# A GRU with an expert-choice layer on one Trainium2 core: the threshold search unrolled, its rounds refilled, its ties summed in one PSUM tile

## The chip, the cores and the metric

The kernel runs on one core of a Trainium2 chip. A core has a matrix engine (PE, or TensorE; its weight loads are shown as PEld), a vector engine (DVE, VectorE), an activation engine (ACT, ScalarE), a general engine (POOL, GpSimd), a queue engine (SP, SyncE) and 16 DMA engines that all the queues share. The engines run side by side and wait for each other through semaphores. The metric is the device time of one execution in microseconds (us), given as the median of three runs.

## The reference

A GRU cell runs over 256 rows of 16 sequences, with width D = 512. Its hidden states are the tokens of an expert-choice layer: each of 16 experts takes the 256 tokens (one in 16) with the highest softmax score, all of them go through one matrix, and the result, weighted by the score, is added to the input.

```python
gi = x @ W_ih + b_ih;  gh = h @ W_hh + b_hh
r = sigmoid(i_r + h_r);  z = sigmoid(i_z + h_z);  n = tanh(i_n + r * h_n)
h_new = (1.0 - z) * n + z * h                       # 256 steps, one after another
...
S = softmax(xf @ router_w + router_b, axis=-1)      # 4096 tokens, 16 experts
G, idx = top_k(S.T, 256)                            # ties go to the lower token index
out = einsum('ekh,hd->ekd', xf[idx], expert_w) + expert_b
y = zeros(...).at[idx.reshape(-1)].add(G[..., None] * out)
return x + y
```

Since all experts share one matrix, the kernel computes `tok @ expert_w + expert_b` for every token, and multiplies each token by the sum of the scores with which experts chose it.

## The kernel before

**Recurrence.** The first 1024 us or so are the 256 steps. A step is 64 matmul records of the recurrence on PE, in two halves, tanh on ACT, the gate arithmetic on DVE; PE fills its time with the input projections of later steps, with router matmuls and with expert matmuls.

**Tokens.** They lie in 32 tiles of 128 tokens by 512. An **expert unit** is a quarter of one 128-deep slice of one tile's expert product: one unit is 128 columns, 16 units make a tile. `expert(units, widest)` (L908 to L926) issues the next units in order, on PE's queue; four units at a quarter boundary go as one 512-wide group. Tiles 12 to 15 are computed in pairs by `paired` (56 units), tiles 16 to 30 follow with 16 units each, and `last_tile` does tile 31 in two halves. A plain tile starts by waiting for `ffn_preset` (L921): ACT has copied the bias into its PSUM bank (`preset_ffn`, L518 to L524). ACT moves nine finished tiles out of PSUM into SBUF (`store_ffn`, L526 to L537), so that their banks come free; the others stay in PSUM until the end.

**The search.** Top-k is done as a threshold search on the score's bits. Seven rounds find the upper 16 bits, eight the lower 16. A round r is a chain over three engines:

- DVE counts two candidates (L1378, each a pass over 512 columns and an accumulator read), ACT counts the third (`count_third`, L666 to L669);
- PE sums the counts per expert with a small matmul (`sum_counts`, L1038 to L1041, matmul at L1034), waiting for ACT's count (`cnt_act`) and DVE's (`cnt_own`);
- DVE compares (`reach`, L1394), makes new candidates (L1405), moves the threshold (L1399) and counts again; while PE works, it prepares steps and bases (`prepare`, L1382 to L1389).

Behind every sum PE issues nine units, so that it has work while DVE and ACT count. On DVE, rounds 1 to 6 are a hardware loop of three turns (L1416) and rounds 8 to 13 another (L1454), two rounds in a turn. The first round's counts are taken quarter by quarter (`count_first`, L1304 to L1312), the first three during the recurrence, the last right after the last softmax; each quarter's scores are first copied to an array of upper halves (L1302), which is what is counted.

Between the two halves, and again at the end, ACT makes one more count (`count_beyond`, L671 to L675) and PE sums it (`sum_beyond`, L1043 to L1047). ACT also does, round by round, one preset or one store (L677 to L701).

**Ties.** After the last round DVE marks scores that equal the threshold, runs a prefix sum over 512 columns (L1468), and takes the number of ties per segment, `R`. PE sums `R` over all groups of an expert and over the groups before, in two sums (L1071 and L1072). DVE subtracts (`others`, L1481), scans (`scan_b`, L1483), subtracts again (`fit`, L1484), and compares each token's rank with what fits (L1492). PE sums the chosen scores into token weights (L1078), a pair of quarters at a time.

**The end.** DVE makes `result = product * weight + x` for all 32 tiles in the order `OUT_ORDER` (`add_x`, L1518 to L1530), SP and ACT issue the stores in turn, and the last tile goes in halves (L1548, L1550). In `OUT_ORDER` eleven places (`PSUM_PLACES`) hold tiles read from PSUM.

Each engine's order is written out by hand; nothing is scheduled by a planner.

Of the kernel before, what the change touches and what calls it, by code (L numbers as in the profile page):

```python
# [5 lines left out]
def gru_expert_choice_kernel(nc, x, cond, w_ih, w_hh, b_ih, b_hh, router_w, router_b, expert_w, expert_b, out):  # L6
# [85 lines left out]
    PSUM_PLACES = [0, 1, 2, 4, 9, 14, 19, 23, 28, 30, 31]  # L92
# [19 lines left out]
    with ctx:  # L112
# [100 lines left out]
        before = sb("before", [P, P], F16)  # L213
        group_of = sb("group_of", [P, NI])
# [20 lines left out]
        R = sb("R", [P, SEG], F16)  # L235
        others = sb("others", [P, 1 + SEG])
        scan_b = sb("scan_b", [P, SEG])
# [9 lines left out]
        R_total_ps = gates[1][1][:, 0:SEG]  # L247
        R_before_ps = gates[1][1][:, SEG:2 * SEG]
# [98 lines left out]
        cnt_act = sem("cnt_act")  # L347
        first_own = sem("first_own")
# [79 lines left out]
        def _(pool):  # L428
# [19 lines left out]
            then_step(nc.gpsimd.memset(before[:, :], 0.0))  # L448
            then_step(nc.gpsimd.memset(group_of[:, :], 1.0))
# [3 lines left out]
            by_group = before[:, :].rearrange("p (j h e) -> p j h e", j=J, h=2)  # L453
            for j in range(J):
# [12 lines left out]
        def _(act):  # L467
# [140 lines left out]
            def count_first_third(g):  # L608
                cols = slice(g * P, (g + 1) * P)
                act.wait_ge(cand_ready, 1)  # L610
                act.wait_ge(key_ready, g + 1)
                nc.scalar.activation(junk_first[:, 0:P], upper[:, cols], ACT.Sign, bias=cand[:, 2:3],
# [64 lines left out]
            for r in range(1, UPPER_ROUNDS + LOWER_ROUNDS + 1):  # L677
# [10 lines left out]
                elif r % 2 and r <= 11:  # L688
                    preset_ffn(PLAIN + r // 2)
                elif r <= 10:  # L690
                    store_ffn(IN_LOOP + r // 2 - 2)
                elif r == 12:
                    store_ffn(PLAIN)
                    preset_ffn(PLAIN + BANKS)
                elif r == 13:
                    store_ffn(PLAIN + 1)
                elif r == 14:
                    preset_ffn(PLAIN + BANKS + 1)
                else:
                    store_ffn(PLAIN + 2)  # L700
# [872 lines left out]
```

## Time and profile before

| | us |
|---|---|
| median of 3 runs (lowest, highest) | 1099.16 (1098.94, 1100.22) |
| the profiled execution | 1098.95 |
| its span in the trace | 1096.8 |
| PE busy | 1085.3 (99%) |
| DVE busy | 857.9 (78%) |
| ACT busy | 411.7 (38%) |
| granted PE clock | 0.998 of full speed |

The profiled execution lies 2.15 us above its span, and 0.21 us below the median. PE's busy time is an upper bound: matmuls are pipelined, and the end of one is modelled. The last 70 us, from 1027 us of the span on, hold the search (15 rounds, to 1061), the ties (to 1067), and then the 32 tile results with their stores. The chain of waits runs through PE for 94% of the span; in the search it runs through DVE.

### The profile page before, as it was taken

The page shows a single profiled execution, that of the slowest core. Times are in us where ns is not written, and L with a number is a line of the kernel's source. Part 1 is how long each engine was busy: PE and PEld are TensorE (multiplying, and loading weights), DVE is VectorE, ACT ScalarE, POOL GpSimd, SP SyncE. Part 2 cuts the span into 40 slices and gives each one's busy share as a digit, 9 for nine tenths or more (in the row PEclk, how much of TensorE's full clock was granted, in tenths as well). Part 3 has the DMA queues.
Part 4 walks back from the last instruction along what each step waited for, and adds up shares of the span by engine and source line. Part 5 has one row for each costly group of instructions (what it writes and reads, how often), then busy time and mean ns, then how long its engine had stood idle before and what let it go on. Part 6 is the DMA issues. An engine that isn't in the chain of part 4 may idle for free.

```text
span 1096.8 us, 60944 instructions
## 1 busy us (share of the span) xinstructions
PE 1085.3 (99%) x26728; PEld 895.2 (82%) x26728; DVE 857.9 (78%) x4603; ACT 411.7 (38%) x1658; POOL 6.9 (1%) x31
## 2 busy tenths in 40 slices
PE   8999999999999999999999999999999999999998
PEld 5788888888888888888888888888888888888742
DVE  5788777877777877787777778778788777777897
ACT  2333333433333433333333334343334333333461
POOL 2000000000000000000000000000000000000000
PEclk9999999999999999999999999999999999999999
DMA  7311000000000000000000000000000000000359
GB/s 255 90 22 23 13 13 13 7 10 13 14 13 13 14 13 9 8 13 13 13 13 14 13 9 8 13 14 13 13 13 14 7 10 14 3 4 4 113 161 307
DMA packets 80446, 36.78 MB, mean 34 GB/s; under 512 B 70051, under 2 KB 70307, under 8 KB 80182
## 3 DMA queue, kind: packets, MB, share of 16 engines
q1 hardware_dynamic: 77840, 28.79, 10.7%
q8 instruction: 209, 3.42, 1.3%
q10 hardware_dynamic: 2342, 4.11, 1.1%
q14 instruction: 55, 0.45, 0.1%
HBM read 24.49 MB, written 8.39 MB: 30 GB/s over the span
## 4 chain that ended last, share of the span: by engine, by line
PE 94%; DVE 3%; DMA 1%; issue 0%; SPq 0%; ACT 0%; DVEq 0%
PE gates L805 60%; PE gates L742 26%; PE ffn_ps L869 3%; PE gates L923 2%; DMA whh<-in_L_cond_W_hh 1%; DVE wih L1378 1%; PE gates L901 1%; PE log_ps L958 1%; PE ffn_ps L923 0%; PE gates L935 0%; DVE reached L1394 0%; SPq L375 0%; PE log_ps L1034 0%; PE ffn_ps L901 0%; SPq L378 0%
## 5 line engine op out<-in xcount | busy, mean ns | idle before, releaser
L805 PE MATMUL gates<-whh,tok 128*16 128x192 f32 x16384 | 713.9, 326 | 3.1 <-DVE tok L1187 2.0
L805 PEld LDWEIGHTS gates<-whh,tok 128*16 128x16 f32 x16384 | 566.2, 124 | 101.0 <-DVE tok L1187 3.9
L511 ACT ACTIVATE th<-gates 128x128 f32<-128x128 f32 x512 | 140.0, 274 | 340.8 <-PE gates L805 340.6
L1162 DVE SCALAR_TENSOR_TENSOR u<-th,gates 128x64 f32<-128x64 f32 x512 | 113.2, 221 | 166.4 <-ACT th L511 166.2
L516 ACT ACTIVATE n_t<-v 128x64 f32<-128x64 f32 x512 | 131.5, 257 | 278.2 <-DVE v L1166 278.2
L742 PE MATMUL gates<-wih,xS 128*32 128x192 f32 x3024 | 146.2, 326 | 0.0
L1178 DVE STREAM_TRANSPOSE nT<-n_t 128x64 f32<-128x64 f32 x512 | 123.6, 241 | 0.0
L1169 DVE STREAM_TRANSPOSE zT<-th 128x64 f32<-128x64 f32 x512 | 121.9, 238 | 0.0
L1166 DVE SCALAR_TENSOR_TENSOR v<-u,gates 128x64 f32<-128x64 f32 x512 | 113.1, 221 | 8.8
L742 PEld LDWEIGHTS gates<-wih,xS 128*32 128x32 f32 x3024 | 99.9, 110 | 21.1
L1187 DVE SCALAR_TENSOR_TENSOR tok<-new_n,z_h 128x32 f32<-128x32 f32 x512 | 110.1, 215 | 8.7
L1174 DVE SCALAR_TENSOR_TENSOR z_h<-zT,half_h 128x32 f32<-128x32 f32 x512 | 98.6, 193 | 17.6
L742 PE MATMUL gates<-wih,xT 128*32 128x192 f32 x2016 | 105.3, 326 | 0.0
L1182 DVE SCALAR_TENSOR_TENSOR new_n<-zT,nT 128x32 f32<-128x32 f32 x512 | 96.7, 189 | 8.8
L742 PEld LDWEIGHTS gates<-wih,xT 128*32 128x32 f32 x2016 | 66.6, 110 | 13.4
L1206 DVE TENSOR_SCALAR half_h<-tok 128x64 f32<-128x64 f32 x255 | 57.6, 226 | 8.7
L742 PE MATMUL gates<-w_sums,xT 128*32 128x192 f32 x1008 | 52.6, 326 | 0.0
L742 PE MATMUL gates<-w_sums,xS 128*32 128x192 f32 x1008 | 52.6, 326 | 0.0
L476 ACT ACTIVATE gates<-bias 128x256 f32<-128x256 f32 x128 | 47.8, 374 | 0.0
L923 PE MATMUL gates<-we,tok 128*32 128x128 f32 (+1 forms) x648 | 44.7, 419 | 0.0
L742 PEld LDWEIGHTS gates<-w_sums,xS 128*32 128x32 f32 x1008 | 33.3, 110 | 7.7
L742 PEld LDWEIGHTS gates<-w_sums,xT 128*32 128x32 f32 x1008 | 33.3, 110 | 7.6
(198 smaller groups left out, 615.9 us busy)
## 6 DMA issues: line engine op xcount, KB each, us to landing
x_in<-in_x SPq DMA_DIRECT2D x248, 32.0 KB, 2.1
out<-tok SPq DMA_DIRECT2D x16, 256.0 KB, 4.2
xs<-in_x SPq DMA_DIRECT2D x14, 256.0 KB, 3.6
out<-tok ACTq DMA_DIRECT2D x13, 256.0 KB, 4.5
wih<-in_L_cond_W_ih SPq DMA_DIRECT2D x4, 768.0 KB, 7.7
whh<-in_L_cond_W_hh SPq DMA_DIRECT2D x4, 768.0 KB, 13.3
whh<-in_x SPq DMA_DIRECT2D x12, 256.0 KB, 3.6
we<-in_L_ffn_expert_w SPq DMA_DIRECT2D x4, 256.0 KB, 2.7
```

What stands on the lines that cost most here:

```text
L511: nc.scalar.activation(th[a][:, :, :].rearrange("p g c -> p (g c)"), gates[t // S % PAIRS][a][:, R_:HN], ACT.Tanh, scale=0.5).then_inc(th_ ...
L516: nc.scalar.activation(n_t[a][:, :], v[a][:, :], ACT.Tanh).then_inc(n_ready[a], 1)
L742: mm = nc.tensor.matmul(ps[Q * j:Q * (j + 1), IN:HN].rearrange("b (g k c) -> b g k c", g=G, k=KH), rows(k), columns(k, j), start=False, st ...
L805: mm = nc.tensor.matmul(gates[t // S % PAIRS][a][Q * j:Q * j + rows, R_:GC].rearrange("b (g k c) -> b g k c", g=G, k=KH), columns, by_tile ...
L923: mm = nc.tensor.matmul(bank(n)[Q * j:Q * (j + 1), cols], tile(n)[:, kc * P + Q * j:kc * P + Q * (j + 1)], we[:, kc, cols], start=False, s ...
L1162: V.scalar_tensor_tensor(u[a][:, :], th[a][:, 0, :], 1.0, ps[a][:, HN:GC], ALU.add, ALU.mult).then_inc(u_ready[a], 1)
L1166: V.scalar_tensor_tensor(v[a][:, :], u[a][:, :], 0.5, ps[a][:, IN:R_], ALU.mult, ALU.add).then_inc(v_ready[a], 1)
L1169: V.transpose(zT[a][:, :, :].rearrange("p k q -> p (k q)"), th[a][:, 1, :]).then_inc(zT_ready[a], 1)
L1174: V.scalar_tensor_tensor(z_h[a][:, :, :], zT[a][:, :, rows], 1.0, half_h[:, chunks[a], :], ALU.add, ALU.mult)
L1178: V.transpose(nT[a][:, :, :].rearrange("p k q -> p (k q)"), n_t[a][:, :]).then_inc(nT_ready[a], 1)
L1182: V.scalar_tensor_tensor(new_n[a][:, :, :], zT[a][:, :, rows], 1.0, nT[a][:, :, rows], ALU.subtract, ALU.mult).then_inc(new_n_ready[a], 1)
L1187: V.scalar_tensor_tensor(by_chunk[:, chunks[a]], new_n[a][:, :, :], -0.5, z_h[a][:, :, :], ALU.mult, ALU.add).then_inc(h_ready[a], 1)
```

## The change

Six things change.

1. Both hardware loops of the search are unrolled on DVE.
2. PE issues ten units in a round instead of nine, through `fill_round`: all but one, then the wait for ACT's next count, then the last. `sum_counts` waits for DVE's count alone.
3. In the first quarter counts, the last quarter is counted where the scores lie (every second 16-bit half), by DVE and by ACT; the copy of the upper halves follows the counts.
4. Ties: a second mask, `behind`, is the transposed order of `before`; both products are summed into one PSUM tile, of `R` and of `R` shifted by one segment. DVE scans that tile directly: two subtractions go.
5. ACT counts `beyond` ahead of `side` in the last round, and the stores and presets of rounds 10 to 15 are spread anew; the units around `sum_beyond` and the ties become 8 and 2, 6 and 6 (from 8 and 6, 8 and 6).
6. `PSUM_PLACES` changes, and the router bias is added in step 22 instead of step 16.

```diff
-    LAST_UNITS, SOFTMAX_UNITS, ROUND_UNITS = [3, 6, 4, 5], 17, 9
-    BEYOND_UNITS, TIE_UNITS = [[7, 5], [8, 6]], [8, 6]
+    LAST_UNITS, SOFTMAX_UNITS, ROUND_UNITS = [3, 6, 4, 5], 17, 10
+    BEYOND_UNITS, TIE_UNITS = [[7, 5], [8, 2]], [6, 6]
-    PSUM_PLACES = [0, 1, 2, 4, 9, 14, 19, 23, 28, 30, 31]
+    PSUM_PLACES = [0, 1, 2, 3, 7, 12, 17, 22, 27, 30, 31]
...
+                    if j:
+                        then_step(fill(by_group_behind[:, 0:j, hi, :], [j], p))
+                    if hi == 1:
+                        then_step(fill(by_group_behind[:, :, 0, :], [J], p))
...
             def count_third(r, key):
                 act.wait_ge(cand_ready, r)
+                if r == 2:
+                    act.wait_ge(key_ready, NG)
...
-                elif r % 2 and r <= 11:
+                elif r % 2 and r <= 9:
                     preset_ffn(PLAIN + r // 2)
                 elif r <= 10:
                     store_ffn(IN_LOOP + r // 2 - 2)
+                    if r == 10:
+                        preset_ffn(PLAIN + BANKS - 1)
+                elif r == 11:
+                    store_ffn(PLAIN)
                 elif r == 12:
-                    store_ffn(PLAIN)
                     preset_ffn(PLAIN + BANKS)
+                    store_ffn(PLAIN + 1)
                 elif r == 13:
-                    store_ffn(PLAIN + 1)
-                elif r == 14:
                     preset_ffn(PLAIN + BANKS + 1)
                 else:
-                    store_ffn(PLAIN + 2)
-                    preset_ffn(PLAIN + BANKS + 2)
+                    store_ffn(PLAIN + r - 12)
+                    preset_ffn(PLAIN + BANKS + r - 12)
+            count_beyond(1, lower)
...
-            count_beyond(1, lower)
-            store_ffn(IN_PSUM - 2)
-            preset_ffn(IN_PSUM + BANKS - 2)
...
+            def fill_round(units, third):
+                expert(units - 1, widest=4)
                 pe.wait_ge(cnt_act, third - 1)
+                expert(1)
+
+            def sum_counts(r):
                 pe.wait_ge(cnt_own, r - 1)
                 sum_by_expert(cnt_ps, cnt[:, :]).then_inc(cnt_all, 1)
...
-            sum_by_expert(R_total_ps, R[:, :])
-            sum_by_expert(R_before_ps, R[:, :], before).then_inc(R_summed, 1)
+            for j in range(J):
+                for mask, of in ((behind, R_earlier), (before, R)):
+                    mm = nc.tensor.matmul(ties_ps[Q * j:Q * (j + 1), :], mask[:, Q * j:Q * (j + 1)], of,
+                                          start=(mask is behind), stop=(mask is before), skip_group_check=True)
+            mm.then_inc(R_summed, 1)
...
-                count = V.tensor_scalar(junk_first[:, (c + 1) * P:(c + 2) * P], upper[:, cols], cand[:, c:c + 1], None, ALU.is_ge,
+                key = S_halves[:, cols, 1] if g == NG - 1 else upper[:, cols]
+                count = V.tensor_scalar(junk_first[:, (c + 1) * P:(c + 2) * P], key, cand[:, c:c + 1], None, ALU.is_ge,
...
-                if t == 2 * TT:
+                if t == 3 * TT - 2:
...
+            copy_upper(NG - 1)
+            dve.wait_ge(key_ready, NG)
...
-            with dve.Fori(0, (UPPER_ROUNDS - 1) // 2) as q:
+            for q in range((UPPER_ROUNDS - 1) // 2):
...
-            with dve.Fori(0, (LOWER_ROUNDS - 1) // 2) as q:
+            for q in range((LOWER_ROUNDS - 1) // 2):
...
-            link(V.tensor_tensor(others[:, 1:], R_total_ps, R[:, :], ALU.subtract))
-
-            link(V.tensor_tensor_scan(scan_b[:, :], zeros[:, :], others[:, 0:SEG], need[:, 0:1], ALU.add, ALU.subtract))
-            link(V.tensor_tensor(fit[:, :], scan_b[:, :], R_before_ps, ALU.subtract))
+            dve.wait_ge(soft, need_set)
+
+            link(V.tensor_tensor_scan(fit[:, :], zeros[:, :], ties_ps, need[:, 0:1], ALU.add, ALU.subtract))
```

PE's order in rounds 8 and 9, before. Rows of 32x3 are the sums of counts; rows of 32x128 and 32x512 are expert units (4 matmuls each for one unit and for four).

```order
L1034 MATMUL log_ps<-cnt,same_expert 32x3 [waits cnt_own,cnt_act]
L1034 MATMUL log_ps<-cnt,same_expert 32x3 x3
L923 MATMUL gates<-we,tok 32x128 x8
L923 MATMUL gates<-we,tok 32x512 x4
L923 MATMUL gates<-we,tok 32x128 x12
L1034 MATMUL log_ps<-cnt,same_expert 32x3 [waits cnt_own,cnt_act]
L1034 MATMUL log_ps<-cnt,same_expert 32x3 x3
L923 MATMUL gates<-we,tok 32x128 x4
L923 MATMUL gates<-we,tok 32x512 x4
L923 MATMUL gates<-we,tok 32x512 [waits ffn_preset]
```

And now, from the sum of round 8 to the sum of round 9:

```order
L1048 MATMUL log_ps<-cnt,same_expert 32x3 [waits cnt_own]
L1048 MATMUL log_ps<-cnt,same_expert 32x3 x3
L937 MATMUL gates<-we,tok 32x512 x8
L937 MATMUL gates<-we,tok 32x128 [waits ffn_preset]
L937 MATMUL gates<-we,tok 32x128 x3
L937 MATMUL gates<-we,tok 32x128 [waits cnt_act]
L937 MATMUL gates<-we,tok 32x128 x3
L1048 MATMUL log_ps<-cnt,same_expert 32x3 [waits cnt_own]
```

The fifth plain tile (tile 20) starts with unit 120. Before, that was the sixth unit behind the sum of round 9; now it is the ninth behind the sum of round 8, and its wait for `ffn_preset` stands ahead of the sum of round 9.

DVE's order from the first row of the tie count to the comparisons, before:

```order
L1469 TENSOR_TENSOR R<-wih 128x64 [waits soft]
L1472 SCALAR_TENSOR_TENSOR wih<-wih 128x512 [waits side_ready]
L1474 TENSOR_SCALAR need<-log_ps,need_base 128x1 [waits cnt_all]
L1481 TENSOR_TENSOR others<-gates,R 128x64 [waits half_taken,half_added,xs_loaded3,R_ready,xs_loaded2,R_summed,xs_loaded1,xs_loaded0]
L1483 SCALAR_TENSOR_TENSOR scan_b<-zeros,need,others 128x64 [waits soft]
L1484 TENSOR_TENSOR fit<-scan_b,gates 128x64 [waits soft]
L1492 TENSOR_TENSOR wih<-wih,fit 128x16x8 [waits soft]
```

And now:

```order
L1508 TENSOR_TENSOR R_padded<-wih 128x64 [waits soft]
L1511 SCALAR_TENSOR_TENSOR wih<-wih 128x512 [waits side_ready]
L1513 TENSOR_SCALAR need<-log_ps,need_base 128x1 [waits cnt_all]
L1522 SCALAR_TENSOR_TENSOR fit<-zeros,need,gates 128x64 [waits half_added,half_taken,R_ready,xs_loaded3,R_summed,xs_loaded2,soft,xs_loaded1,xs_loaded0]
L1530 TENSOR_TENSOR wih<-wih,fit 128x16x8 [waits soft]
```

One instruction stands where three stood, and the wait for PE's sum of ties (`R_summed`) has moved to it.

## Rows read from the trace of the kernel before

**Rows 1.** Windows, the search: busy us of each engine, clock, DMA.
```profile
core 0: us, PE busy (x) PEld busy (x) DVE busy (x) ACT busy (x) POOL busy (x), PEclk, DMA share, GB/s
1027.30:1063.20 35.90, 33.18 (x700) 17.84 (x692) 33.19 (x194) 22.23 (x53) 0.00 (x0) 1.00 0.68 200
```
**Rows 2.** Timeline, PE: start us, us, engine line op, names [idle before].
```profile
1029.35 0.19 PE L1034 MATMUL log_ps<-cnt,same_expert 128*32 128x3 f16 x4
...
1036.43 0.19 PE L1034 MATMUL log_ps<-cnt,same_expert 128*32 128x3 f16 x4
...
1038.94 0.19 PE L1034 MATMUL log_ps<-cnt,same_expert 128*32 128x3 f16 x4 [0.35 <-DVE wih L1378]
...
1041.22 0.19 PE L1034 MATMUL log_ps<-cnt,same_expert 128*32 128x3 f16 x4
...
1044.56 0.19 PE L1034 MATMUL log_ps<-cnt,same_expert 128*32 128x3 f16 x4 [0.23 <-DVE wih L1378]
...
1046.94 0.19 PE L1034 MATMUL log_ps<-cnt,same_expert 128*32 128x3 f16 x4 [0.21 <-DVE wih L1378]
...
1060.80 0.19 PE L1034 MATMUL log_ps<-cnt,same_expert 128*32 128x3 f16 x4
1060.83 1.93 PE L923 MATMUL ffn_ps<-we,tok 128*32 128x128 f32 x40
```
**Rows 3.** Timeline, DVE: the comparison behind a sum.
```profile
1036.91 0.16 DVE L1394 SCALAR_TENSOR_TENSOR reached<-log_ps,target 128x3 f32<-128x3 f32 x1 [0.35 <-PE log_ps L1034]
...
1047.18 0.16 DVE L1394 SCALAR_TENSOR_TENSOR reached<-log_ps,target 128x3 f32<-128x3 f32 x1
```
**Rows 4.** Timeline, ACT: count and preset behind the sum at 1044.56.
```profile
1045.37 0.72 ACT L668 ACTIVATE wih<-wih,cand 128x512 uint16<-128x512 uint16 x1 [1.02 <-DVE cand L1405]
...
1046.09 0.58 ACT L524 ACTIVATE gates<-be 128x512 f32<-128x512 f32 x1
```
**Rows 5.** Counts on DVE by source line: ns minimum/median/maximum.
```profile
L1378 DVE TENSOR_SCALAR_CACHE_REDUCE wih<-upper_bits,cand x12: 737/741/745, 1027.8 to 1040.3; 128x512 uint16<-128x512 uint16 x12
```
```profile
L1309 DVE TENSOR_SCALAR_CACHE_REDUCE junk_first<-upper_bits,cand x8: 304/340/346, 466.7 to 1026.6; 128x128 uint16<-128x128 uint16 x8
```
**Rows 6.** Timeline, DVE: the ties.
```profile
1063.41 0.28 DVE L1469 TENSOR_TENSOR R<-wih 128x64 f16<-128x64 f32 x1
...
1064.21 0.21 DVE L1474 TENSOR_SCALAR need<-log_ps,need_base 128x1 f32<-128x1 f32 x1
1065.01 0.23 DVE L1481 TENSOR_TENSOR others<-gates,R 128x64 f32<-128x64 f32 x1 [0.59 <-PE gates L1034]
1065.28 0.35 DVE L1483 TENSOR_TENSOR_SCAN scan_b<-zeros,need,others 128x64 f32<-128x64 f32 x1
1065.66 0.22 DVE L1484 TENSOR_TENSOR fit<-scan_b,gates 128x64 f32<-128x64 f32 x1
1065.92 0.49 DVE L1492 TENSOR_TENSOR wih<-wih,fit 128x128 f32<-128x128 f32 x2
```
**Rows 7.** Timeline, ACT: side and beyond after the last round.
```profile
1061.76 0.72 ACT L704 ACTIVATE wih<-scores_by_expert,edge 128x512 f32<-128x512 f32 x1 [0.61 <-DVE edge L1464]
1062.39 0.71 ACT L674 ACTIVATE wih<-wih,beyond 128x512 uint16<-128x512 uint16 x1
1063.00 0.19 ACT L674 ACTIVATION_READ_ACCUMULATOR wih<-wih,beyond 128x1 f16 x1
```
**Rows 8.** Timeline, DVE: tile 30 and the first half of tile 31.
```profile
1090.20 0.75 DVE L1528 SCALAR_TENSOR_TENSOR tok<-gates,weight,w_sums 128x512 f32<-128x512 f32 x1 [0.67 <-PE gates L923]
1091.92 0.48 DVE L1548 SCALAR_TENSOR_TENSOR w_sums<-gates,weight,w_sums 128x256 f32<-128x256 f32 x1 [0.98 <-PE gates L935]
```
**Rows 9.** DMA issues from 1090 us (KB each, us to landing); windows near the end.
```profile
out<-tok ACTq DMA_DIRECT2D x1, 256.0 KB, 4.5
...
out<-w_sums SPq DMA_DIRECT2D x1, 128.0 KB, 2.3
```
```profile
1094.50:1095.50 1.00, 0.00 (x0) 0.00 (x0) 0.00 (x0) 0.00 (x0) 0.00 (x0) 1.00 0.19 54
```
**Rows 10.** The page: the recurrence's matmuls and PE's idle time before them.
```profile
L805 PE MATMUL gates<-whh,tok 128*16 128x192 f32 x16384 | 713.9, 326 | 3.1 <-DVE tok L1187 2.0
```

More of the change, by code:

```diff
@@ L213, in gru_expert_choice_kernel @@
         before = sb("before", [P, P], F16)
+        behind = sb("behind", [P, P], F16)
         group_of = sb("group_of", [P, NI])
@@ L234, in gru_expert_choice_kernel @@
         need = sb("need", [P, 1])
-        R = sb("R", [P, SEG], F16)
-        others = sb("others", [P, 1 + SEG])
-        scan_b = sb("scan_b", [P, SEG])
+        R_padded = sb("R_padded", [P, 1 + SEG], F16)
+        R, R_earlier = R_padded[:, 1:], R_padded[:, 0:SEG]
         fit = sb("fit", [P, SEG])
@@ L448, in _ @@
             then_step(nc.gpsimd.memset(before[:, :], 0.0))
+            then_step(nc.gpsimd.memset(behind[:, :], 0.0))
             then_step(nc.gpsimd.memset(group_of[:, :], 1.0))
@@ L453, in _ @@
             by_group = before[:, :].rearrange("p (j h e) -> p j h e", j=J, h=2)
+            by_group_behind = behind[:, :].rearrange("p (j h e) -> p j h e", j=J, h=2)
             for j in range(J):
@@ L610, in count_first_third @@
                 act.wait_ge(cand_ready, 1)
-                act.wait_ge(key_ready, g + 1)
-                nc.scalar.activation(junk_first[:, 0:P], upper[:, cols], ACT.Sign, bias=cand[:, 2:3],
+                if g < NG - 1:
+                    act.wait_ge(key_ready, g + 1)
+                    key = upper[:, cols]
+                else:
+                    act.wait_ge(scored, 1)
+                    key = Sc.bitcast(U16).rearrange("p (n two) -> p n two", two=2)[:, cols, 1]
+                nc.scalar.activation(junk_first[:, 0:P], key, ACT.Sign, bias=cand[:, 2:3],
                                      accum_out=cnt_first[:, g, 2:3]).then_inc(first_act, 1)
@@ L1046, in sum_beyond @@
                 sum_by_expert(cnt_beyond_ps[half], cnt_beyond[:, half:half + 1]).then_inc(cnt_all, 1)
-                expert(BEYOND_UNITS[half][1], widest=4)
             pe.wait_ge(masks_ready, 1)
@@ L1300, in soften, with copy_upper @@
                 if i == 6:
-                    link(V.transpose(Sc[:, cols], by_token_scores[:, :]))
-                    V.tensor_copy(upper[:, cols], S_halves[:, cols, 1]).then_inc(key_ready, 1)
+                    turned = V.transpose(Sc[:, cols], by_token_scores[:, :])
+                    if g == NG - 1:
+                        turned.then_inc(scored, 1)
+                        dve.wait_ge(scored, 1)
+                    else:
+                        link(turned)
+                    if g < NG - 1:
+                        copy_upper(g)
+            def copy_upper(g):
+                cols = slice(g * P, (g + 1) * P)
+                V.tensor_copy(upper[:, cols], S_halves[:, cols, 1]).then_inc(key_ready, 1)
             def count_first(g, c):
                 cols = slice(g * P, (g + 1) * P)
-                dve.wait_ge(key_ready, g + 1)
+                if g < NG - 1:
+                    dve.wait_ge(key_ready, g + 1)
                 dve.wait_ge(cand_ready, 1)
-                count = V.tensor_scalar(junk_first[:, (c + 1) * P:(c + 2) * P], upper[:, cols], cand[:, c:c + 1], None, ALU.is_ge,
+                key = S_halves[:, cols, 1] if g == NG - 1 else upper[:, cols]
+                count = V.tensor_scalar(junk_first[:, (c + 1) * P:(c + 2) * P], key, cand[:, c:c + 1], None, ALU.is_ge,
                                         ALU.add, accum_out=cnt_first[:, g, c:c + 1])
@@ L1439, in _ @@
             V.memset(no_prefix, 0.0)
-            V.memset(others[:, 0:1], 0.0)
+            V.memset(R_padded[:, 0:1], 0.0)
             dve.wait_ge(cand_ready, UPPER_ROUNDS + 1)
@@ L1473, in _ @@
             dve.wait_ge(cnt_all, ALL_ROUNDS + 2)
-            mark(V.tensor_scalar(need[:, :], cnt_beyond_ps[1], -0.5, need_base[:, :], ALU.mult, ALU.add))
+            need_set = mark(V.tensor_scalar(need[:, :], cnt_beyond_ps[1], -0.5, need_base[:, :], ALU.mult, ALU.add))
             for p in range(4):
```

23 lines of the change are left out of this document (12 added, 11 removed).

## The prediction

> **What bounds the kernel now.** I began with the page. PE is busy for 99% of the span, and its only idle time in the recurrence is 3.1 us over 256 steps [rows 10]. So the change can only act behind the recurrence. Next came the windows. In the search, from 1027.3 to 1063.2, PE counts as busy for 33.18 of 35.90 us and DVE for 33.19 [rows 1]: two engines hand work to each other, and both are short of full by 2.7 us. Then PE's timeline, for the distance from one sum of counts to the next. Where no loop boundary lies between, it is 2.28 us (1038.94 to 1041.22). From 1036.43 to 1038.94 it is 2.51, and PE then stood idle for 0.35 us until DVE's count came [rows 2]. DVE's timeline shows why: the comparison starts 0.24 us behind its sum in the plain case (1046.94, 1047.18), but 0.48 us behind the sum at 1036.43, where the loop turns [rows 2, 3]. Hence in the search DVE's chain sets the pace, and PE's expert units are filler. At the end it is the other way round: DVE waits for PE before tile 30 (0.67 us) and before the first half of tile 31 (0.98 us) [rows 8].
>
> The total of expert units is the same. PE therefore ends earlier by what it no longer idles. That is two things: how much earlier the search and the ties end (call it D), and how many units were moved from behind them into the idle time.
>
> **Unrolling.** Sums 2 to 7 span 1029.35 to 1041.22, 11.87 us for five rounds; at 2.28 each this would be 11.40: 0.47 us less. Sums 9 to 15 span 1046.94 to 1060.80, 13.86 us; six times 2.28 is 13.68: 0.18 less [rows 2]. Sum 0.65 us. It can't be much more, since the plain round stays, and it can be nothing if code without a loop stalls elsewhere.
>
> The Trainium skill ("Advanced Engine Details and Errata", Control Flow Timing) gives a compare-and-branch about 108 ns. By that figure four boundaries would be worth an estimated 0.43 us instead of 0.65. The trace agrees for a lower boundary and shows twice as much for the upper one that I quote; the rows decide.
>
> **Ten units in a round.** Eight units take 1.93 us with a tail of 0.19 that the sums show too, so a unit is (1.93 - 0.19) / 8 = 0.218 us [rows 2]. Ten are 2.18, and 0.03 for the sum ahead of them makes 2.21: under 2.28, by 0.07. DVE stays the pace-maker, barely. ACT's count, now waited for before the tenth unit, ends some 1.7 us behind a sum (1045.37 + 0.72 + 0.19 for the accumulator, less 1044.56) [rows 2, 4, 7], while the tenth unit is due at 1.98. So this wait is free. Behind it on PE's queue stand only the last unit and the sum.
>
> **One round gets a new wait.** The order rows show tile 20 starting as the ninth unit behind sum 8, with a wait for `ffn_preset`. PE gets there at 0.03 + 8 x 0.218 = 1.77 us behind the sum. ACT issues that preset in its round 9, right behind the count: 1046.09 + 0.58 = 1046.67, which is 2.11 us behind sum 8 [rows 2, 4]. Its place on ACT has not changed. PE stands still for 0.34 us, then does two units (0.44) and sums at about 2.60, instead of 2.38 before (1044.56 to 1046.94). DVE has long finished and waits too. Cost: 0.22 to 0.3 us, I take 0.25. The other plain tiles start at units 72, 88, 104, 136, 152, 168, 184 and 200, and each preset of theirs is issued at least a round ahead or right at the round's start; I cost these at nothing, and each that I have wrong costs up to the same 0.34.
>
> **The last quarter counted in place.** The copy leaves the way to the first comparison, but comes back just before `prepare`, which the comparison needs in order. The transposed scores, two counts, one copy and four preparations stand on DVE before and after; only the order differs. Sum 1 may come a little earlier, the comparison doesn't. I take 0, between -0.1 and +0.2. Is a strided 16-bit read slower? The dense count takes 340 ns for 128 elements and 741 for 512 [rows 5]: 401 ns for 384, 1.04 ns an element.
>
> The Trainium skill ("VectorE: DVE Perf Modes", What auto-detection actually checks) has a double rate for 16-bit tensors with step 1, by which the dense count would be fast and the strided one lose it. The trace shows no such rate in the dense count, so nothing is lost; by the rule, two counts would each lose an estimated 0.07 us.
>
> **Ties.** All times from sum 15 at s = 1060.80. Before, DVE has `need` started at s + 3.41, waits 0.59 us for PE's sums of R, and goes through `others`, the scan and `fit` to the comparisons at s + 5.12 [rows 6]. PE was late since ACT made `side` ahead of `beyond`: the count ended at 1063.00 + 0.19, s + 2.39 [rows 7], and then six units (1.31) stood ahead of the sum of R. Now ACT's `beyond` starts where `side` started, s + 0.96, and ends at about s + 1.77; PE has its eight units done by s + 1.77, sums, does two units by s + 2.25 and is ready for R, which DVE writes from s + 2.61 to s + 2.89 [rows 6]. R is summed by s + 3.25, `side` ends by s + 2.5, and neither is late for DVE. `need` ends at s + 3.62, the scan starts at s + 3.66; from the start of the scan to the next instruction it took 0.38 before (1065.28 to 1065.66). The comparisons start at s + 4.04: 1.08 us earlier. Reading PSUM in the scan instead of SBUF is not in the trace; `others` read PSUM and cost 0.27 from start to start, so I bound it by 0 and 0.2.
>
> So D = 0.65 - 0.25 + 0 + 1.08 = 1.48 us, from 0.9 to 1.9.
>
> **Units moved.** Ten instead of nine in 13 rounds are 13 more; the second `sum_beyond` has four fewer and the ties two fewer behind it: 7 more by the time of the weights, 7 x 0.218 = 1.5 us less for PE behind them. PE ends 1.48 + 1.5 = 3.0 us earlier. DVE's tile results start D earlier and had 0.67 + 0.98 = 1.65 us to spare for the 1.5 that PE gains on them [rows 8]: enough by 0.15. The new `PSUM_PLACES` keep the tiles in PSUM at places where their products and the bank presets are ready.
>
> **Stores.** These start only D earlier. Before, a 256 KB store near the end took 4.5 us to land and the last, of 128 KB, 2.3 [rows 9]: the queue was full, and had drained for the last one. From 1094.5 to 1095.5 the DMA engines were 0.19 busy [rows 9], so there is about 0.8 us of air ahead of the last half, plus what the late tile 30 opened before it. The stores can thus end 1.48 + 0.8 = 2.3 to 2.9 us earlier, PE 3.0. The later one counts. I take 2.7.
>
> **Other parts.** The bias add moves from step 16 to step 22, beside work with slack both times, as PE's idle time there is nothing; POOL builds one mask more in the first 20 us, needed 1000 us later. ACT's store and preset in one round add up to 0.72 + 0.19 + 2 x 0.58 = 2.07 us, less than 2.28. Each at nothing.
>
> **Sum.** 1098.95 - 2.7 = 1096.25 for an execution like the profiled one, which lies 0.2 below the median: 1096.5 us. A measurement of this kernel can tell about 0.2%, 2.2 us, from no change; 1096.96 is that border.
>
> **Rivals.**
>
> *The stores set the end.* If the queue of stores is full to its last byte, the end moves by D alone, plus nothing for the units moved: 1099.16 - 1.5 = 1097.7. For it: 4.5 us of landing. Against: the 0.19 window. Chance 0.2, and in steps between.
>
> *PE becomes the bound of the search.* The margin is 0.07 us a round. If ten units and a sum take 2.35, 11 rounds lose 0.07 each, 0.8 us of D, but PE then idles for nothing: PE ends at the same total, stores 0.8 later, giving 1097.3. For it: narrow units with a wait in between. Chance 0.12.
>
> *Fetching unrolled code (slower).* DVE runs 14 rounds of straight code in a stretch in which loads keep the DMA engines 0.68 busy [rows 1]. If the code comes in pieces over the same engines, and each piece takes as long as a queued transfer (4.5 us [rows 9]) with DVE standing, two such stops cost 9.0 us, of which 2.7 are covered: 1099.16 + 6.3 = 1105.5. It decides from one stop on (+1.8). Against: DVE and PE both run straight code through the whole recurrence and PE through this very search, and the idle times in the rows are below 0.6 us. Chance 0.05.
>
> The Trainium skill ("Advanced Engine Details and Errata", ISA Cache) speaks for this rival: it describes a store of two lines of 256 instructions each, which a two-round loop fits and unrolled code leaves. No row here shows such a stop.
>
> *The change doesn't do what it says.* Loop boundaries cost what they cost for another reason, the straight code keeps them: D is 0.65 smaller, 1097.1. Chance 0.05. The forecast itself keeps 0.58, with a range of its own from 1095.7 to 1097.0.
>
> **Chances.** Faster by over 0.2%: nearly all of the forecast, and near a third of the rivals that end at 1097: 0.62. Within 0.2%: 0.32. Slower: 0.06. The range for 8 in 10 is 1095.4 to 1098.6.
>
> **What would show it.** In the profile after: sums 2.28 us apart everywhere but from 8 to 9, where PE's weight loads wait for ACT's preset and the distance is about 2.6; the comparisons 4.04 us behind sum 15; PE's last matmul 3.0 us earlier; DVE without idle time before tile 30; the last store landing in more than 2.3 us. The forecast is wrong if sums come 2.35 or more apart, if other presets are waited for, or if DVE shows a stop with no engine named.

## The result, and the profile after

| us | before | after |
|---|---|---|
| median (lowest, highest) of 15 executions each, taken side by side | 1099.28 (1098.87, 1100.22) | 1095.98 (1095.10, 1097.74) |
| the profiled execution | 1098.95 | 1096.32 |
| its span | 1096.8 | 1094.6 |
| PE busy | 1085.3 | 1081.6 |

The kernel became faster: ratio after to before 0.9971, 95% interval 0.9964 to 0.9978, which is 3.2 us; the medians lie 3.3 us apart. The forecast was 1096.5.

The sums of counts and two rows at which PE waited (PE's timeline after; start, duration, idle time before in brackets; answers to [rows 2]):

```profile
1029.28 0.19 PE L1048 MATMUL log_ps<-cnt,same_expert 128*32 128x3 f16 x4
...
1036.00 0.19 PE L1048 MATMUL log_ps<-cnt,same_expert 128*32 128x3 f16 x4
1038.23 0.19 PE L1048 MATMUL log_ps<-cnt,same_expert 128*32 128x3 f16 x4
1040.44 0.19 PE L1048 MATMUL log_ps<-cnt,same_expert 128*32 128x3 f16 x4
...
1043.71 0.19 PE L1048 MATMUL log_ps<-cnt,same_expert 128*32 128x3 f16 x4
1045.86 0.64 PE L937 MATMUL gates<-we,tok 128*32 128x128 f32 x16 [0.20 <-ACT gates L531]
1046.32 0.19 PE L1048 MATMUL log_ps<-cnt,same_expert 128*32 128x3 f16 x4
...
1059.65 0.19 PE L1048 MATMUL log_ps<-cnt,same_expert 128*32 128x3 f16 x4
...
1062.61 0.22 PE L1094 MATMUL gates<-R_padded,behind 128*32 128x64 f16 x4 [0.52 <-DVE R_padded L1508]
```

Without a loop, neighbouring sums are 2.20 to 2.24 us apart (1036.00, 1038.23, 1040.44), not 2.28. Once, from sum 3 to sum 4, it is 2.29. Sum 2 to sum 15 takes 30.37 us; before it took 31.45. One stretch is long: 1043.71 to 1046.32, 2.61, with PE waiting for ACT's preset.

The ties on DVE's timeline after (answers to [rows 6]), and then DVE around tile 31 (answers to [rows 8]):

```profile
1062.28 0.28 DVE L1508 TENSOR_TENSOR R_padded<-wih 128x64 f16<-128x64 f32 x1
...
1063.07 0.21 DVE L1513 TENSOR_SCALAR need<-log_ps,need_base 128x1 f32<-128x1 f32 x1
1063.41 0.35 DVE L1522 TENSOR_TENSOR_SCAN fit<-zeros,need,gates 128x64 f32<-128x64 f32 x1
1063.80 0.49 DVE L1530 TENSOR_TENSOR wih<-wih,fit 128x128 f32<-128x128 f32 x2
...
1065.28 0.75 DVE L1566 SCALAR_TENSOR_TENSOR tok<-gates,weight,whh 128x512 f32<-128x512 f32 x1
...
1087.31 0.75 DVE L1566 SCALAR_TENSOR_TENSOR tok<-gates,weight,w_sums 128x512 f32<-128x512 f32 x1
1088.29 0.48 DVE L1586 SCALAR_TENSOR_TENSOR w_sums<-gates,weight,w_sums 128x256 f32<-128x256 f32 x1 [0.23 <-PE gates L949]
```

The comparisons start 4.15 us behind sum 15 (before 5.12), and the first tile result at 1065.28; before it started at 1067.39. That is D: 2.11 us. Tile 30 has no idle time ahead of it.

The last stores after (issues from 1088 us, us to landing), and the DMA engines to the end (windows of 1 us; answer to [rows 9]):

```profile
out<-tok ACTq DMA_DIRECT2D x1, 256.0 KB, 5.1
...
out<-w_sums SPq DMA_DIRECT2D x1, 128.0 KB, 3.6
```
```profile
1091.00:1092.00 1.00, 0.00 (x0) 0.00 (x0) 0.00 (x0) 0.00 (x0) 0.00 (x0) 1.00 1.00 310
1092.00:1093.00 1.00, 0.00 (x0) 0.00 (x0) 0.00 (x0) 0.00 (x0) 0.00 (x0) 0.86 0.91 294
1093.00:1094.00 1.00, 0.00 (x0) 0.00 (x0) 0.00 (x0) 0.00 (x0) 0.00 (x0) 0.50 0.30 100
```

The gap ahead of the last half is gone: the DMA engines are full to 1092 and 0.91 busy to 1093, and the last 128 KB take 3.6 us where they took 2.3. PE's last tile starts at 1086.31 (before 1089.94), the last store is issued at 1090.53 (before 1094.16). Both are 3.63 earlier; 1.3 of it is given back in the queue.

### The profile page after: what moved, and what is told of

It is laid out like the page before. It is cut to its first block, busy times and chain, and to the rows that moved or that the text cites. A ratio compares the mean times of both kernels' runs of the same rounds, so it can differ in the third digit from the quotient of the medians.

```text
span 1094.6 us, 60966 instructions
## 1 busy us (share of the span) xinstructions
PE 1081.6 (99%) x26752; PEld 892.5 (82%) x26752; DVE 857.2 (78%) x4601; ACT 411.3 (38%) x1658; POOL 15.5 (1%) x42
## 3 DMA queue, kind: packets, MB, share of 16 engines
q8 instruction: 209, 3.42, 1.3%
## 4 chain that ended last, share of the span: by engine, by line
PE 96%; DVE 1%; DMA 1%; SPq 0%; ACT 0%; issue 0%; DVEq 0%
PE gates L819 60%; PE gates L756 26%; PE ffn_ps L883 3%; PE gates L937 3%; DMA whh<-in_L_cond_W_hh 1%; PE gates L915 1%; PE ffn_ps L937 1%; PE log_ps L972 1%; PE gates L949 0%; DVE wih L1417 0%; SPq L376 0%; PE ffn_ps L915 0%; DVE u L1186 0%; SPq L379 0%; DVE wih L1507 0%
```

## The experiments

The comparison is with 1095.98 for the changed kernel, and with its trace. The kernel before, run beside them, had medians of 1099.24 to 1099.35. A profiled execution can be compared from sum 2 on; where it begins differs (last section).

**Experiment 1: the wait for ScalarE's count.** Ten units stay, the wait moves back to the sum.

```diff
                 expert(units - 1, widest=4)
-                pe.wait_ge(cnt_act, third - 1)
                 expert(1)
+                pe.wait_ge(cnt_act, third - 1)
```


> The changed kernel, with ScalarE's count waited for right ahead of the sum again (ten units, then both waits). Theory A: the second wait standing between the last unit and the sum costs about 0.06 us in each round, since after the change the distance from one sum to the next is 2.21 us where it was 2.28. Then the plain rounds come at 2.26 to 2.30 us here, sum 15 about 0.7 us later, and the whole 0.7 us slower. Rival: the rounds are shorter because PE no longer runs dry ahead of the sum (ten units fill it), and where the wait stands is worth nothing: 2.21 us and the same time as the changed kernel within 0.2 us.

Measured 1096.75 (ratio to before 0.9978, 0.9968 to 0.9987). PE's timeline of this kernel:

```profile
1036.24 0.19 PE L1048 MATMUL log_ps<-cnt,same_expert 128*32 128x3 f16 x4
1038.52 0.19 PE L1048 MATMUL log_ps<-cnt,same_expert 128*32 128x3 f16 x4
1040.79 0.19 PE L1048 MATMUL log_ps<-cnt,same_expert 128*32 128x3 f16 x4
```

The round is 2.27 to 2.28 again, and sum 2 to sum 15 takes 30.96: 0.59 us lost, about 0.05 in a plain round. Theory A held, though ACT's count had ended 0.76 us ahead of the sum (its accumulator read starts 0.95 ahead of it and takes 0.19). The profile shows no idle time for this wait. Where it sits shows from DVE's side: the last thing that the sum needs is DVE's second accumulator read, which in the changed kernel and in this one starts at

```profile
1038.09 0.09 DVE L1417 DVE_READ_ACCUMULATOR wih<-upper_bits,cand 128x1 f16 x1
```
```profile
1038.29 0.08 DVE L1417 DVE_READ_ACCUMULATOR wih<-upper_bits,cand 128x1 f16 x1
```

The sums behind them are at 1038.23 and 1038.52: 0.14 and 0.23 us later. With the wait at the sum it is 0.23 or 0.24 in every plain round, here and in the kernel before. With the wait moved it is 0.14 in a kernel with nine units (experiment 3) and 0.13 to 0.18 with ten, but for sum 9 behind the preset's stop. So the wait costs 0.09 us where it stands ahead of the sum, and ten units take part of that back.

**Experiment 2: the wait moved in the kernel before**, which keeps its loops and its nine units.

```diff
-            expert(ROUND_UNITS, widest=4)
+            fill_round(ROUND_UNITS, 2)
```


> The kernel before (loops, nine units) with ScalarE's count waited for ahead of the last unit and nothing else. By theory A each of 13 rounds is 0.06 to 0.08 us shorter, 2.19 to 2.21 us in the plain ones, sum 15 0.8 to 1.0 us earlier and the end 0.8 us. Rival: the shorter round needs the unrolled code as well: less than 0.3 us.

Measured 1098.59 (0.9994, 0.9985 to 1.0003), 0.65 under the kernel before and within the noise; the profiled execution was the slowest, 1100.16. Sum 2 to sum 15 went from 31.45 to 30.85, 0.60 less. But it is not the same gain in each round: seven rounds fell from 2.27 or 2.28 to 2.18 or 2.19 (1029.50 to 1031.68), 0.09 each, and the six in which a loop starts, turns or ends stayed where they were (2.54, 2.51, 3.34, 2.38, 2.38, 2.38). DVE's timeline at an upper boundary shows why, first before, then here:

```profile
1036.40 0.15 DVE L1389 SCALAR_TENSOR_TENSOR base<-steps,thr_away 128x1 f32<-128x1 f32 x1
1036.91 0.16 DVE L1394 SCALAR_TENSOR_TENSOR reached<-log_ps,target 128x3 f32<-128x3 f32 x1 [0.35 <-PE log_ps L1034]
```
```profile
1036.47 0.15 DVE L1394 SCALAR_TENSOR_TENSOR base<-steps,thr_away 128x1 f32<-128x1 f32 x1
1036.98 0.16 DVE L1399 SCALAR_TENSOR_TENSOR reached<-log_ps,target 128x3 f32<-128x3 f32 x1 [0.35 <-PE log_ps L1034]
```

The comparison starts 0.51 us behind the last preparation both times, though the sum (1036.43, 1036.41) came 0.23 and 0.14 behind the counts. Both rows name PE, but here DVE's own loop turn sets the comparison, and an earlier sum gains nothing. Experiment 1 found nearly the same total by other parts: about 0.05 in each of eleven plain rounds, with ten units.

**Experiment 3: nine units in the changed kernel.**

```diff
-    LAST_UNITS, SOFTMAX_UNITS, ROUND_UNITS = [3, 6, 4, 5], 17, 10
+    LAST_UNITS, SOFTMAX_UNITS, ROUND_UNITS = [3, 6, 4, 5], 17, 9
```


> The changed kernel with nine expert units in a round, everything else new. Theory A (the wait moved ahead of the last unit gives the shorter round): the rounds stay at 2.20 to 2.22 us though PE runs dry ahead of each sum, the round from sum 8 to 9 falls to 2.3, and PE's last matmul comes 13 x 0.214 = 2.8 us later less 0.35, near 1092.5 us; the end then is PE's again, about 1.5 us later than the changed kernel. Rival (a PE without gaps gives the shorter round): the rounds go back to 2.27 us, and everything comes 0.7 us later still.

Measured 1097.72 (0.9984, 0.9974 to 0.9993): 1.7 us slower than ten units; the profiled execution was the slowest, 1100.15. The sums come 2.18 to 2.19 apart, closer than with ten, so PE without gaps is not what shortened the rounds. Ten units make the round 0.035 us longer than nine. PE's last tile starts at 1090.44, 4.1 later than with ten. 13 units of 0.218 left for the end are 2.8. Sum 15 is 1.34 later: this execution's sum 2 came 0.68 later, the rounds are 0.64 shorter in all, and there is a stop of 1.30:

```profile
1032.14 0.18 PE L1048 MATMUL log_ps<-cnt,same_expert 128*32 128x3 f16 x3
1033.63 0.18 PE L1048 MATMUL log_ps<-cnt,same_expert 128*32 128x3 f16 x1 [1.30 <-issue]
```

PE stands between the third and the fourth matmul of one sum, and the row names no engine that it waited for. More on it below.

**Experiment 4: the loops put back** in the changed kernel.

```diff
-            for q in range((UPPER_ROUNDS - 1) // 2):
+            with dve.Fori(0, (UPPER_ROUNDS - 1) // 2) as q:
```
(and the same for the lower rounds)

> The changed kernel with both hardware loops on VectorE again. My price: 0.65 us, at two boundaries of the upper loop (0.23 to 0.26 us each) and two of the lower (about 0.1 each); sum 15 comes 0.5 to 0.7 us later and the end 0.5 to 0.7 us. Rival: with ten units PE covers part of a boundary: sum 15 under 0.3 us later.

Measured 1097.18 (0.9982, 0.9973 to 0.9992). DVE's timeline at two loop turns:

```profile
1031.93 0.16 DVE L1433 SCALAR_TENSOR_TENSOR reached<-log_ps,target 128x3 f32<-128x3 f32 x1 [0.38 <-PE log_ps L1048]
...
1036.64 0.16 DVE L1433 SCALAR_TENSOR_TENSOR reached<-log_ps,target 128x3 f32<-128x3 f32 x1 [0.35 <-PE log_ps L1048]
```

The sums ahead of them were at 1031.38 and 1036.09: 0.55 from sum to comparison, where the round after it has 0.24. Rounds with an upper boundary take 2.49 and 2.50, with a lower one 2.39 and 2.35. Sum 2 to 15 takes 31.27, 0.90 more than unrolled: more than the 0.65 expected, and the rival failed.

**Experiment 5: unrolling alone**, in the kernel before.

```diff
-            with dve.Fori(0, (UPPER_ROUNDS - 1) // 2) as q:
+            for q in range((UPPER_ROUNDS - 1) // 2):
```


> The kernel before with the two loops unrolled and nothing else. Price as in the prediction: sum 15 0.65 us earlier (0.23 to 0.26 at each of two upper boundaries, 0.1 at each of two lower ones), PE's last matmul as much, the end 0.5 to 0.7 us earlier. Putting the loops back into the changed kernel cost 0.90 us up to sum 15; by that rival 0.9 us here.

Measured 1098.56 (0.9993, 0.9984 to 1.0002), 0.7 under the median before and within the noise. Sum 2 to 15 takes 30.98, 0.47 less; but one of PE's sums in it is stretched:

```profile
1031.96 0.50 PE L1034 MATMUL log_ps<-cnt,same_expert 128*32 128x3 f16 x4
1034.53 0.19 PE L1034 MATMUL log_ps<-cnt,same_expert 128*32 128x3 f16 x4
```

Four matmuls that take 0.19 took 0.50, and the round 2.57. Without these 0.30 the unrolling would be worth an estimated 0.77. In the kernel before the same sum took 0.38, which cost nothing, since a loop boundary lay behind it. The plain round stays at 2.27 to 2.28, so it is not what shortened the rounds after.

**Experiment 6: the late preset issued a round earlier.**

```diff
+                elif r == 9:
+                    pass
...
+                    if r == 8:
+                        preset_ffn(PLAIN + BANKS - 2)
```


> The changed kernel with the bias preset of tile 20 one round earlier on ScalarE, behind the store of round 8, so that PE doesn't stop ahead of sum 9. Theory: the distance from sum 8 to sum 9 falls from 2.61 us to 2.35, everything behind it comes 0.25 us earlier, the stores too, and so the end: -0.25 us (-0.0 to -0.4), under what times alone can tell. Rival: the end doesn't follow, since something else sets it.

Measured 1095.96 (0.9969, 0.9958 to 0.9980). PE's sums 8 and 9:

```profile
1043.74 0.19 PE L1052 MATMUL log_ps<-cnt,same_expert 128*32 128x3 f16 x4
1046.01 0.19 PE L1052 MATMUL log_ps<-cnt,same_expert 128*32 128x3 f16 x4
```

The distance falls from 2.61 to 2.27, and sum 2 to 15 from 30.37 to 30.00. The stop was 0.34 to 0.37 us. The median did not move. In the trace PE's last tile and the last store (1090.24) start 0.29 earlier; a gain of 0.3 is less than these executions scatter, so whether the end follows stays open.

**Experiment 7: the old tie sums** in the changed kernel.

```diff
-            link(V.tensor_tensor_scan(fit[:, :], zeros[:, :], ties_ps, need[:, 0:1], ALU.add, ALU.subtract))
+            link(V.tensor_tensor(others[:, 1:], R_total_ps, R, ALU.subtract))
+            link(V.tensor_tensor_scan(scan_b[:, :], zeros[:, :], others[:, 0:SEG], need[:, 0:1], ALU.add, ALU.subtract))
+            link(V.tensor_tensor(fit[:, :], scan_b[:, :], R_before_ps, ALU.subtract))
...
```
(and on PE the two sums of the kernel before)

> The changed kernel with the old ties: two sums on PE, then subtract, scan, subtract on VectorE; the new order on ScalarE (beyond ahead of side) and the two units behind it stay. Of my 1.08 us for the ties, two instructions less are 0.26 + 0.26 us by their starts before, and the rest came from PE's sum being ready in time. Expected: from sum 15 to the comparisons 4.15 + 0.5 = 4.65 us, first tile result 0.5 us later, end 0.5 us later. Rival: the whole gain hangs on the single scan, and the comparisons come over 0.9 us later.

Measured 1096.76 (0.9979, 0.9968 to 0.9989). DVE's timeline:

```profile
1063.27 0.23 DVE L1522 TENSOR_TENSOR others<-gates,R_padded 128x64 f32<-128x64 f32 x1
1063.54 0.35 DVE L1523 TENSOR_TENSOR_SCAN scan_b<-zeros,need,others 128x64 f32<-128x64 f32 x1
1063.92 0.22 DVE L1524 TENSOR_TENSOR fit<-scan_b,gates 128x64 f32<-128x64 f32 x1
1064.17 0.49 DVE L1532 TENSOR_TENSOR wih<-wih,fit 128x128 f32<-128x128 f32 x2
```

Sum 15 is at 1059.51, so the comparisons start 4.66 behind it: 0.51 for the two subtractions. `others` shows no wait here. So of the 0.97 that the ties gained, 0.51 is the two subtractions. The other 0.46 is left to ACT's and PE's new order, which no run had by itself.

**Experiment 8: the copy back ahead of the counts** in the last quarter.

```diff
-                key = S_halves[:, cols, 1] if g == NG - 1 else upper[:, cols]
+                key = upper[:, cols]
...
```
(the copy goes ahead of the counts, and ACT counts the copy too)

> The changed kernel with the last quarter copied to the array of upper halves first and counted there, by VectorE and ScalarE, as before. I had counted this part at nothing: the first comparison then starts at the same distance behind the transposed scores, within 0.1 us (before 1.54, changed kernel 1.44), and the run is the same. Rival: the copy ahead of the counts costs its 0.23 us.

Measured 1096.79 (0.9976, 0.9967 to 0.9986), 0.8 over the changed kernel, with intervals that overlap. The trace supports less. From the transposed scores to the first comparison it has 1.55 us (1026.65, 1028.20), after 1.44 (1025.89, 1027.33), before 1.54; to sum 2 it has 3.53, 3.39 and 3.58. So counting in place is worth 0.11 to the comparison and 0.14 to sum 2. The rest of the difference in medians isn't in these rows; this execution began its recurrence 0.76 later (the second step at 24.38 against 23.62).

**Experiments 9 to 11: do the stores set the end?** Four of the last tile results (places 24 to 27) are computed and not stored, so these rows of the output are missing. After:

```diff
+                if i in (24, 26):
+                    continue
...
-                if i % 2:
+                if i % 2 and i not in (25, 27):
```


> The changed kernel without the stores of places 24 to 27 (1 MB of the output is not written). Leaving out places 12 to 15 only lowered the landing time of the last half from 3.6 to 3.0 us, since the queue filled again behind the hole. Theory S: with a late hole the queue is empty at the end, the last half lands 2.3 to 2.5 us after its issue, and the run is about 1.2 us shorter than the changed kernel, PE at its place. Rival: no more than 0.3 us shorter.

Before, with the same edit:

> The kernel before without the stores of places 24 to 27 (1 MB of the output is not written). Theory S: before the change the queue had drained by the last store (2.3 us to landing), PE set the end: under 0.2 us shorter. Rival: the stores already set the end before, and it is shorter by as much as the changed kernel is without the same stores.

And after with places 12 to 15 left out in their stead:

> The changed kernel without the stores of the results at places 12 to 15 (1 MB of the output is not written). Theory S: after the change the store queue sets the end (the last half lands 3.6 us after its issue, where it took 2.3 before); with four stores fewer it lands after 2.3 us again, and the run is 1.2 to 1.5 us shorter, PE's last matmul at the same place. Rival P: PE and the last result set the end, and the landing time is a side effect: no change within 0.3 us.

| not stored | us | ratio to before | last landing | median against the kernel with all stores |
|---|---|---|---|---|
| after, 24 to 27 | 1095.35 | 0.9963 (0.9950, 0.9975) | 2.3 | -0.6 |
| before, 24 to 27 | 1099.22 | 1.0000 (0.9990, 1.0009) | 2.3 | 0 |
| after, 12 to 15 | 1095.72 | 0.9966 (0.9954, 0.9979) | 3.0 | -0.3 |

The last landing after, without places 24 to 27 (issues from 1088 us, us to landing):

```profile
out<-w_sums SPq DMA_DIRECT2D x1, 128.0 KB, 2.3
```

Before, these stores cost nothing. After, the same edit takes the last landing from 3.6 to 2.3 and the span from 1094.6 to 1093.2. With places 12 to 15 left out the hole fills again: the DMA engines were 0.74 to 0.83 busy from 1076 to 1082 (windows of 2 us), and 0.98 and more from 1084 on. There the median fell by 0.3, where 1.2 to 1.5 was expected. Without places 24 to 27 it came out 0.6 shorter, where theory S wanted 1.2. Part of the rest is outside the span, where this kernel spends 2.0 to 2.1 us and the changed one 1.7 to 1.8; the spans' medians differ by 0.95 (1094.2, 1093.25). The medians' difference is about the size of the scatter, so this rests on the spans and the landings. One landing alone is a weak witness: in experiment 2, near the kernel before, the last half took 3.8 us in the one execution that was profiled. Within that, stores did not set the end before, and they hold it back now.

**Experiment 12: two tile results ahead of each second comparison**, with experiment 6 in it, so that the stores start sooner.

```diff
-    BEYOND_UNITS, TIE_UNITS = [[7, 5], [8, 2]], [6, 6]
+    BEYOND_UNITS, TIE_UNITS = [[7, 5], [8, 2]], [6, 9]
...
             add_x(0)
+            add_x(1)
             choose(QUARTERS[2])
             choose(QUARTERS[3])
-            add_x(1)
+            add_x(2)
+            add_x(3)
             take_weights(slice(2, 4))
...
```

> The changed kernel with the preset of tile 20 a round earlier, and on VectorE the results of places 0 and 1 ahead of the choice of the second pair of quarters, those of places 2 and 3 ahead of its weights (nine units on PE ahead of that pair's sums, not six). Since the stores set the end of the changed kernel, earlier first stores should count: 0.37 us from the preset as measured, and 0.2 to 0.4 from stores 1 to 3 coming 0.2 to 0.4 us earlier. Expected 0.5 to 0.8 us under the changed kernel: 1095.3. Rival: the queue's rate, not its start, sets its end, and only the 0.37 remain.

Measured 1097.02 (0.9979, 0.9970 to 0.9988), worse than the 1095.96 it was built on. Its search takes 31.49 us from sum 2 to 15 instead of 30.00, and PE's timeline says why:

```profile
1030.95 0.82 PE L941 MATMUL gates<-we,tok 128*32 128x128 f32 x19
1032.89 0.53 PE L941 MATMUL gates<-we,tok 128*32 128x128 f32 x11 [1.12 <-issue]
```

A stop of 1.12 us, again with no engine named, again at 1032; the other 0.37 of the difference lies in the same two rounds, from sum 2 to sum 4. Behind sum 15 the edit did a little: the third result starts 7.35 us behind it (1061.10, 1068.45), after 7.55 (1059.65, 1067.20). What it is worth without the stop stays open. The four fastest of its eleven executions, 1095.47 to 1096.33, are no faster than those of experiment 6 (1095.07 to 1096.91).

**What the two stops share.** The profile lists the queue that fetches code ("instruction") in DMA windows. Queue q8 moved 3.42 MB in 209 packets of 16 KB; PE has 26752 matmuls and as many weight loads, and 3.42 MB over these is 64 bytes each, so I take this for PE's code. The window from 1028.50 to 1028.75 of the kernel after, and then that from 1030.00 to 1030.25 of experiment 12:

```profile
q8 instruction: 1, 0.02, 27.5%
```
```profile
q8 instruction: 1, 0.02, 31.1%
```

By windows of 0.25 us the packets start at these times:

| | first | second | third | stop of PE |
|---|---|---|---|---|
| before | 1024.50 | 1028.25 | 1033.00 | none |
| after | 1024.75 | 1028.50 | 1032.50 | none |
| experiment 12 | 1025.50 | 1030.00 | 1034.25 | 1.12, ends at 1032.89 |
| experiment 3 | 1025.25 | 1031.00 | 1034.75 | 1.30, ends at 1033.63 |

In the twelve profiles without such a stop (before, after and experiments 1, 2, 4 to 11) the second packet starts 3.50 to 3.75 us behind the first; in the two with one, 4.5 and 5.75 behind. At 1028 the loads of `x` begin: their first packets come in the window from 1028 to 1029 after, and the engines are 0.84 busy in the next. So in both profiles with a stop, a packet that came 0.75 to 2 us late stands among these loads. That PE ran dry for want of it is not shown. By the rows the packet was over before PE stopped: in experiment 12 it took 1.24 us (31.1% of 16 engines for 0.25 us) from 1030.00 to 1030.25 on, so it ended by 1031.49, and PE stood from 1031.77 to 1032.89. In experiment 3 it ended about when the stop began. The smaller stretches of sum 3 (0.38 before, 0.50 in experiment 5, 0.31 in experiment 10) had no late packet. This is an observation on two executions; no kernel was made to bring the stop about or to remove it.

## Why the prediction was right, and what was off in it

**The mechanism held.** PE's units were filler in the search, all but 0.035 us a round, and PE was the bound behind it. Its end moved by D plus the units moved: 2.11 + 7 x 0.218 = 3.64, and the last tile did start 3.63 earlier. The step was right; D was mis-sized, 2.11 and not 1.48. D by parts, from the transposed scores: to sum 2, 0.19; sums 2 to 15, 1.08; from sum 15 to the first result 0.96; less 0.12 by which this execution's scores came later.

**"So this wait is free" is the term that failed.** Moving it was valued at 0, because ACT's count ends 0.3 us before the tenth unit is due. Ended or not, a wait right ahead of the sum costs 0.09 us in each round that the sum bounds; what takes that time no row shows. Ten units take 0.035 back, and the round is 2.20 to 2.24 and not 2.28. Over sums 2 to 15 the move is worth 0.59 in the changed kernel (experiment 1) and 0.60 in the kernel before (experiment 2).

**Unrolling was 0.65 and is an estimated 0.77 in the kernel before, 0.90 in the changed one** (experiments 5 and 4). A round with an upper boundary takes 2.50 us either way [rows 2], since there the loop turn sets the comparison (experiment 2), while the plain round that it is measured against fell from 2.28 to 2.22; four boundaries at 0.06 more are 0.24. An upper boundary now costs 0.28 us, a lower one 0.13 to 0.17. The Trainium skill ("Advanced Engine Details and Errata", Control Flow Timing) has about 108 ns for a compare-and-branch; by these rows that is near a lower boundary's price and less than half of an upper one's.

**The preset's stop** was to be 0.25, from 0.22 to 0.3, with sums 2.60 apart; they were 2.61 apart, but against a round of 2.27 that is 0.34 (experiment 6). No other preset was waited for, as forecast.

These three make the search: 0.77 + 0.60 - 0.34 = 1.03 of the 1.08 measured; 0.40 had been forecast. The parts are not independent: each loop boundary hides the price of the wait.

**"DVE stays the pace-maker, barely" was wrong by a little.** Its 2.28 held the price of the wait. Without it DVE's chain alone takes 2.18 to 2.19 (nine units, experiment 3), and ten units with their sum, 2.21 by the prediction's own count, take longer: the rounds are 2.22 on average, 0.035 over. So the rival in which PE sets the pace had the right kind and the wrong size, 2.35. That costs less than leaving 13 units to the end (experiment 3).

**Ties:** 1.08 forecast, 0.97 measured to the comparisons. The scan starts 0.34 behind the start of `need` where 0.25 was forecast, and that is nearly all of the miss; half of the gain is the subtractions (experiment 7). **The quarter in place** had been put at 0, between -0.1 and +0.2, and gains 0.11 to the comparison, 0.14 to sum 2 (experiment 8); the rest of the 0.19 in D is left to the wait. In-place counts take 0.342 to 0.346 us, dense ones 0.309 to 0.346: here the stride costs nothing.

**The stores.** The step gave them 2.3 to 2.9 earlier, against 3.0 of PE, and took the later. So it was: PE 3.63, the last landing 2.3 earlier. The rival "the stores set the end" had the right place and the wrong price: D alone (1.5) would have been 1097.7. The "0.8 us of air" was real and was used up.

**The sum.** The forecast took 2.7 off the profiled execution. It moved by 2.63: the span by 2.2, and what lies around the span from 2.15 to 1.72. Over all executions the spans' median moved by 3.0 (from 1097.2, taken from those of the kernel before that ran beside the experiments, to 1094.2) and the median of the times by 3.3; the profiled execution after lies 0.34 above its median. So the agreement is partly luck: PE's lead was 0.6 larger than forecast, the queue of stores took 1.3 of it back and not 0.3, and 0.43 came from around the span, which the sum had left as it was.

**The rival of fetched code** looked for a stop on DVE, and none shows there: in the search after, no idle time on DVE is without an engine named. Nor do the packets of 8 KB in the other code queue, q14, follow the loops: 55 before, 57 after, but 55 too with the loops unrolled (experiment 5) and 56 with them put back (experiment 4). Stops with no engine named came on PE, in two of fourteen profiles, in kernels other than the two compared; that PE's code causes them is the likely reading and not shown. The prediction said that no row showed such a stop; of the kernel before that is still so. The Trainium skill ("Advanced Engine Details and Errata", ISA Cache) has code in cache lines of 16 KB with 256 instructions each; the packets of q8 agree, those of q14 have half that size.

## What to carry to other kernels

A wait that is already satisfied can still have a price, here 0.09 us, where it stands ahead of a short instruction on the critical chain: wait for the count that is done early ahead of the last piece of filler, and keep only the latest one at the sum. Compare distances between repeated rows, not idle times, to find such costs, and compare them round by round: two equal totals came from different rounds here. When the bound at the end moves by 3 us, look at the queue behind it: the air that a late engine left in it is what the change will spend first.

## What the hardware showed that I had not expected

- Executions of one kernel differ before any of this begins. The first half step waits for a weight load by DMA; the second step starts at 23.31 in the trace before, at 24.38 in experiment 8, and in experiment 10 (profiled at 1100.42) the first sum comes 1.5 us later than before, at 1028.21 against 1026.74, without any stop.
- PE stood for 1.1 to 1.3 us with no engine named, in a stretch in which loads fill the DMA engines and in which a packet of code came late. The highest times after, 1097.50 to 1097.74 in three of 15 executions, would fit such a stop; they have no trace, so this is open.
- The time outside the span was 1.72 to 1.79 us in the profiled executions of seven kernels whose last landing took 3.1 us or more, and 2.05 to 2.25 where it took 3.0 or less; in experiment 2 it was 2.16 with a last landing of 3.8. It goes with the kernel more than with the execution: 1.69 to 1.81 in the 15 executions after, 2.06 to 2.18 in 83 of the kernel before. What makes the difference stays open.
